# A four-layer conditioned network: pass change, first stagings, tail, store order and demodulation rearranged

## What is computed

```python
# layers 0 and 1 (attention); s1, s2 are halves of the conditioning
xn = normalise(x * s1)
q_dc = rsqrt(einsum('oi,bi->bo', q_weight**2, s1**2) + 1e-8)      # and k, v, w, u
q, k, v = (xn @ q_weight.T) * q_dc, (xn @ k_weight.T) * k_dc, (xn @ v_weight.T) * v_dc * s2
out = softmax(q @ k.T / 4) @ v
x = x + (out @ w_weight.T) * w_dc + (v @ u_weight.T) * u_dc

# layers 2 and 3 (state space), D_INNER 512, D_STATE 16
xr, gate = split(x @ W_in.T);  xr = xr + cond
xn = layernorm(silu(conv4(xr))) * ln_g + ln_b
Bm, Cm, dt = split(xn @ W_xproj.T)
Ad = 1 - 0.01 * tanh(dt @ W_dt.T + b_dt) * tanh(A_log)
Bd = Bm * min(norm(xn), 1)
for t in range(64):
    h = clip(h * Ad[t] + Bd[t] * xn[t], -10, 10)                  # 64 x 16 x 512
    y[t] = Cm[t] @ h
x = x + ((y + D * xn) * silu(gate)) @ W_out.T
```

## Time and profile before

| | us |
|---|---|
| median of 3 runs | 1900.43 |
| lowest, highest | 1898.62, 1903.49 |
| the profiled execution | 1892.64 |
| its span in the trace | 1890.8 |
| PE / DVE / ACT / POOL busy | 1702.5 / 1654.7 / 1313.4 / 667.1 |
| wait of ACT ahead of `xh` (L880) for the x parts' store, 12 times | 17.8 |
| wait of ACT ahead of `R` (L994) for PE, twice | 13.2 |

### The profile page before, as it was taken

The page is one execution under the profiler, slowest core; times in us unless marked ns, Lnnn a source line. Parts: engine busy times, 40 slices in busy tenths (PEclk is TensorE's granted clock), DMA queues, the critical chain, the costliest instruction groups (busy, mean ns, idle before and its releaser), DMA issues.

```text
span 1890.8 us, 46062 instructions
## 1 busy us (share of the span) xinstructions
PE 1702.5 (90%) x14896; PEld 765.6 (40%) x14896; DVE 1654.7 (88%) x2494; ACT 1313.4 (69%) x2220; POOL 667.1 (35%) x689
## 2 busy tenths in 40 slices
PE   6899899999988999689989998899996899999987
PEld 3555555555553455322222224444452222222243
DVE  3799999999976889989999997569899999999975
ACT  3555455555545888789989991068987899899900
POOL 0223223232321222446656550002225476566400
PEclk9999999999999999799999999999997999899999
DMA  4000000000001334645445658523346454456586
GB/s 153 2 2 0 1 1 30 2 1 0 2 1 78 108 144 177 202 132 160 147 140 189 211 153 253 179 79 140 120 169 204 131 176 145 131 189 216 158 264 237
DMA packets 127189, 228.27 MB, mean 121 GB/s; under 512 B 36085, under 2 KB 61941, under 8 KB 118005
## 3 DMA queue, kind: packets, MB, share of 16 engines
q1 hardware_dynamic: 127064, 226.67, 36.3%
HBM read 143.27 MB, written 83.36 MB: 120 GB/s over the span
## 4 chain that ended last, share of the span: by engine, by line
PE 41%; DVE 24%; ACT 14%; issue 9%; DMA 7%; SPq 3%; DVEq 1%; ACTq 0%
PE PS L1427 9%; PE PS L1410 8%; PE PS L1009 7%; ACT R L994 7%; DVE q L1932 5%; DMA sgp<-sg_d 4%; DVE sm L1564 3%; PE PS L1075 3%; PE PS L1237 3%; DMA xpart_d<-xlo 2%; SPq L328 2%; PE PS L1430 2%; PE PS L1477 2%; ACT ex L724 2%; DVE vare L1505 1%
## 5 line engine op out<-in xcount | busy, mean ns | idle before, releaser
L994 ACT ACTIVATE R<-q,Ast 128x512 f32<-128x512 f32 x1024 | 637.6, 709 | 42.9 <-DVE q L1932 28.1
L1932 DVE SCALAR_TENSOR_TENSOR q<-R,PS 128x512 f32<-128x512 f32 x1008 | 610.0, 676 | 16.8 <-ACT R L994 14.9
L596 POOL TENSOR_TENSOR Uw<-Ub,rowmask 96x512 bf16<-96x512 bf16 x256 | 337.4, 1349 | 188.8 <-PE PS L1410 175.7
L1410 PE MATMUL PS<-xq,Uw 97*128 97x512 bf16 x1024 | 329.1, 397 | 47.2 <-DVE q L1932 39.6
L1427 PE MATMUL PS<-q,Wy 128*32 128x512 f32 x2016 | 283.5, 617 | 1.2 <-DVE q L1932 0.7
L1237 PE MATMUL PS<-X,Win 128*128 (+1 forms) x512 | 239.0, 609 | 4.3 <-DVEq L1715 2.9
L1410 PEld LDWEIGHTS PS<-xq,Uw 97*128 97x128 bf16 x1024 | 85.7, 97 | 367.8 <-DVE q L1932 327.9
L1009 PE MATMUL PS<-xn,Wl 128*128 128x512 f32 x384 | 188.9, 616 | 0.0
L524 POOL TENSOR_TENSOR ex<-ex,rs 128x1024 f32<-128x1024 f32 x32 | 76.9, 2404 | 176.7 <-DVE rs L1567 176.7
L1736 DVE SCALAR_TENSOR_TENSOR acc<-xp,Wc,acc 128x512 f32<-128x512 f32 x192 | 134.6, 748 | 2.5
L1237 PEld LDWEIGHTS PS<-X,Win 128*128 128x128 f32 x512 | 93.1, 192 | 105.2 <-issue 105.2
(11 more groups left out here) (163 smaller groups left out, 2630.4 us busy)
## 6 DMA issues: line engine op xcount, KB each, us to landing
xq<-xpart_d SPq DMA_DIRECT2D x384, 192.0 KB
sg_d<-sg SPq DMA_DIRECT2D x16, 1024.0 KB, 6.7
xn_d<-z SPq DMA_DIRECT2D x16, 1024.0 KB, 5.6
y_d<-ys SPq DMA_DIRECT2D x64, 256.0 KB, 3.9
xnp<-xn_d SPq DMA_DIRECT2D x16, 1024.0 KB, 9.5
sgp<-sg_d SPq DMA_DIRECT2D x16, 1024.0 KB, 12.6
yt<-y_d SPq DMA_DIRECT2D x32, 512.0 KB, 9.1
xpart_d<-xh SPq DMA_DIRECT2D x16, 512.0 KB, 2.9
```

The costliest lines, as they stand in the source:

```text
L596: pl.tensor_tensor(Uw[0:XROWS, h, w, :, :, :], Ub[0:XROWS, w, 0:N, ds(s0, CH)].rearrange("p n t -> p t n").unsqueeze(2).broadcast_to([XROW ...
L994: act.activation(R[:, w, :], q[:, t % 2, w, :], ACT.Relu, scale=Ast[:, h, w, t:t + 1], bias=CLIP).then_inc(ac_r, 1)
L1410: pe.matmul(PS[:, w, :], Uw[0:KROWS, h, w, t, :, :].rearrange("p b n -> p (b n)"), xq[0:KROWS, hb, w, s8 % XT, :], start=True, stop=True). ...
L1932: v.scalar_tensor_tensor(out=q[:, s8 % 2, w, :], in0=R[:, w, :], scalar=2 * CLIP, in1=PS[:, w, :], op0=ALU.min, op1=ALU.subtract).then_inc ...
```

## The change

- **Pass change.** A new buffer `R_end` takes the state after step 63 of pass 0 (ACT's last 4 activations of the pass write it). POOL, no longer DVE, turns it into the clipped state, between `stage(1, 0, 0)` and `stage(1, 0, 1)`. ACT's wait for the last y is gone at the second pass. PE issues the next pass's `inputs` 0 ahead of y 63, `inputs` 1 behind it, and the last y only behind `inputs` 2 of the next pass. At the end of pass 1 DVE still does it in R.
- **First stagings.** POOL waits for `row_r` of the last group ahead of chunk 0's staging (mean rows) and of chunk 1's (deviation rows). PE waits for each `Uw` by itself instead of for all four.
- **Tail.** Most parts of `last_group` come one to two steps later on PE, ACT and DVE. `log_norm` now runs ahead of the switch to the tanh table, so one of the table loads goes.
- **Stores.** In the front the x parts are stored ahead of the B rows, except for group 6.
- **Demodulation.** The second layer's is cut in four, each part in a body (g = 2 to 5) ahead of `largest`; for this DVE's bodies 1 to 4 of the first layer are straight code.

```diff
@@ -193,6 +193,7 @@
 ys = sb("ys", [P, 2, DI], where=scan)
+R_end = sb("R_end", [P, QW, DI], where=scan)
@@ -351,8 +352,8 @@
 store_decay(it, g)
+store_parts(it, g)
 store_b(it, g)
-store_parts(it, g)
@@ -412,14 +413,14 @@
 load_tables(0, (1,))
+store_parts(l * G + QW, QW)
 store_b(l * G + QW, QW)
-store_parts(l * G + QW, QW)
...
 store_decay(l * G + QW + 1, QW + 1)
+store_parts(l * G + QW + 1, QW + 1)
 store_b(l * G + QW + 1, QW + 1)
-store_parts(l * G + QW + 1, QW + 1)
@@ -623,6 +624,8 @@
 for h in range(2):
+    pl.wait_ge(row_r, l * (2 * G) + (2 * AT + 2 * G - 1 + h))
+    alone(pl)
@@ -645,7 +648,13 @@
 alone(pl)
-with pl.Fori(0, CHUNKS // 2) as c2:
+stage(1, 0, 0)
+for p in range(2):
+    pl.wait_ge(ac_r, l * (PASSES * QW * S) + QW * S - QW + 2 * p + 2 + READY)
+    alone(pl)
+    pl.tensor_scalar(R_end[:, 2 * p:2 * p + 2, :], R_end[:, 2 * p:2 * p + 2, :], 2 * CLIP, -CLIP, ALU.min, ALU.add).then_inc(ep_q, 1)
+stage(1, 0, 1)
+with pl.Fori(1, CHUNKS // 2) as c2:
@@ -947,24 +956,24 @@
     std_high(it)
+if n == 2:
     std_middle(it)
-if n in (3, 4):
-    for m in (2 * n - 6, 2 * n - 5):
-        shifted(it, m)
...
     for m in (2 * n - 10, 2 * n - 9):
+        shifted(it, m)
+if n in (7, 8):
+    for m in (2 * n - 14, 2 * n - 13):
         squared(it, m)
-if n == 9:
+if n == 10:
     minus_c(it)
+if n == 11:
     decay_in(it)
-if n == 10:
-    silu_set()
-if n == 11:
-    decay_tanh(it, PS[:, 6, 3 * P:4 * P])
-    logarithm_set()
...
     log_norm(it)
-if n == 16:
+    silu_set()
+if n == 13:
+    decay_tanh(it, PS[:, 6, 3 * P:4 * P])
+if n == 17:
@@ -980,18 +989,18 @@
-def clamp(pi, c2, first, between=None):
+def clamp(pi, c2, first, between=None, end=None):
...
         act.wait_ge(pl_a, cn + 1)
-        if first and h == 0:
+        if first and h == 0 and between:
...
                 act.wait_ge(dv_q, cn * (QW * CH) + QW * t + w + 1 + QW)
-                act.activation(R[:, w, :], q[:, t % 2, w, :], ACT.Relu,
+                act.activation((end if end and (h, t) == (1, CH - 1) else R)[:, w, :], q[:, t % 2, w, :], ACT.Relu,
@@ -999,8 +1008,9 @@
     clamp(pi, c2, c2 == 0, last_group if ps == 0 else None)
-with act.Fori(plain, CHUNKS // 2) as c2:
+with act.Fori(plain, CHUNKS // 2 - 1) as c2:
     clamp(pi, c2, False)
+clamp(pi, CHUNKS // 2 - 1, False, end=R_end if ps == 0 else None)
@@ -1363,23 +1373,23 @@
 it = l * G + G - 1
-if n == 1:
+if n == 3:
...
     spread_out(7, rows3, zb_mm)
-if n == 5:
+if n == 7:
     project_part(it, 2, xd_mm)
-if n == 6:
+if n == 8:
     project_part(it, 0)
-if n == 7:
+if n == 9:
     project_part(it, 1, xw_mm)
-if n == 8:
+if n == 10:
...
         norm(it, m)
-if n == 10:
+if n == 12:
...
     decay(it, PS[:, 6, 3 * P:4 * P])
-if n == 15:
+if n == 16:
@@ -1403,14 +1413,14 @@
         pe.wait_ge(one_in[s8 // 4], l * 32 + 32)
-    if t == 0:
-        pe.wait_ge(pl_u, cn * QW + QW)
     for w in range(QW):
+        if t == 0:
+            pe.wait_ge(pl_u, cn * QW + w + 1)
...
-def y_of(pi, c2, s8, last=False, spare=None):
+def y_of(pi, c2, s8, last=None, spare=None):
@@ -1425,7 +1435,7 @@
 pe.matmul(PS[32 * w:32 * w + 32, 4 + h, :], Wy[:, h, w, t * 32:(t + 1) * 32],
-          R[:, w, :] if last else q[:, s8 % 2, w, :], start=(t == 0), stop=False, skip_group_check=True)
+          last[:, w, :] if last else q[:, s8 % 2, w, :], start=(t == 0), stop=False, skip_group_check=True)
@@ -1435,11 +1445,14 @@
 pi = l * PASSES + ps
-plain = TAIL if ps == 0 else 0
+plain = TAIL if ps == 0 else 1
...
     for s8 in range(1, 9):
-        last_group(c2 * 8 + s8)
-        inputs(pi, c2, s8 + 1, c2 == 0)
+        if ps == 0:
+            last_group(c2 * 8 + s8)
+        inputs(pi, c2, s8 + 1, ps == 0 and c2 == 0)
+        if ps and s8 == 1:
+            y_of(pi - 1, CHUNKS // 2 - 1, 8, last=R_end, spare=(0, 0))
@@ -1448,11 +1461,12 @@
             inputs(pi, CHUNKS // 2 - 1, s8 + 1)
+        elif ps == 0:
+            inputs(pi + 1, 0, 0)
         y_of(pi, CHUNKS // 2 - 1, s8)
-    if ps + 1 < PASSES:
-        inputs(pi + 1, 0, 0)
+    if ps == 0:
         inputs(pi + 1, 0, 1)
-    y_of(pi, CHUNKS // 2 - 1, 8, last=True, spare=(0, 0) if ps + 1 < PASSES else (XB - 1, XT - 1))
+y_of(l * PASSES + PASSES - 1, CHUNKS // 2 - 1, 8, last=R, spare=(XB - 1, XT - 1))
@@ -1607,17 +1621,48 @@
-def demodulation(l):
...
+def all_dco(l):
+    return dco[:, l * 5:l * 5 + 5, :, :].rearrange("p w c b -> p (w c b)")
...
+def dco_step0(l):
     v.wait_ge(dco_g, l + 1)
-    dcv = dco[:, l * 5:l * 5 + 5, :, :].rearrange("p w c b -> p (w c b)")
-    root(dcv, dsq[:, l, :], EPS_DM, dcv, dtm[:, :], dco_r, l * 3)
+    v.scalar_tensor_tensor(out=dtm[:, :], in0=dsq[:, l, :], scalar=EPS_DM, in1=all_dco(l),
+                           op0=ALU.add, op1=ALU.mult).then_inc(dco_r, 1)
...
+def dco_step1(l):
+    v.wait_ge(dco_r, l * 3 + 1)
+    v.scalar_tensor_tensor(out=dtm[:, :], in0=dtm[:, :], scalar=-0.5, in1=all_dco(l),
+                           op0=ALU.mult, op1=ALU.mult).then_inc(dco_r, 1)
...
+def dco_step2(l):
+    v.wait_ge(dco_r, l * 3 + 2)
+    v.scalar_tensor_tensor(out=all_dco(l), in0=dtm[:, :], scalar=1.5, in1=all_dco(l),
+                           op0=ALU.add, op1=ALU.mult).then_inc(dco_r, 1)
...
+def dco_tables(l):
+    v.wait_ge(dco_r, l * 3 + 3)
...
     v.wait_ge(tab_r, l * 2 + 2)
...
+def demodulation(l):
+    dco_step0(l)
+    dco_step1(l)
+    dco_step2(l)
+    dco_tables(l)
...
+def demodulation_piece(l, n):
+    if n == 0:
+        dco_step0(l)
+    if n == 1:
+        dco_step1(l)
+    if n == 2:
+        dco_step2(l)
+    if n == 3:
+        dco_tables(l)
@@ -1657,6 +1702,8 @@
 out_of(it, l, g, 0)
+if l == 0 and g in (2, 3, 4, 5):
+    demodulation_piece(1, g - 2)
@@ -1694,13 +1741,12 @@
 body(l * G, l, 0, 0, (l - 1, G - 1) if l else None, (l, 1), 2)
-with v.Fori(0, 2) as g2:
-    for u in range(2):
-        body(g2 * 2 + (l * G + 1 + u), l, g2 * 2 + (1 + u), 1 - u, (l, g2 * 2 + u),
-             (l, g2 * 2 + (2 + u)), g2 * 2 + (3 + u))
-if l == 0:
-    demodulation(1)
-for g in range(5, G):
+if l:
+    with v.Fori(0, 2) as g2:
+        for u in range(2):
+            body(g2 * 2 + (l * G + 1 + u), l, g2 * 2 + (1 + u), 1 - u, (l, g2 * 2 + u),
+                 (l, g2 * 2 + (2 + u)), g2 * 2 + (3 + u))
+for g in range(5 if l else 1, G):
@@ -1871,22 +1917,24 @@
     inverse_std(it, 6)
+if n == 2:
     std_rest(it)
+if n == 3:
     std_rows(it)
-if n in (2, 3):
-    for m in (2 * n - 4, 2 * n - 3):
+if n in (4, 5):
+    for m in (2 * n - 8, 2 * n - 7):
         gained(it, m, 7)
-if n == 9:
+if n == 11:
     norm_bound(it)
-if n == 13:
+if n == 14:
...
     over_last(it)
-if n == 14:
     inverse_norm(it)
+if n == 15:
...
     carried(it)
-if n == 16:
+if n == 17:
@@ -1954,9 +2002,10 @@
         eight(pi, c2, False, True)
-    for p in range(2):
-        v.wait_ge(ac_r, pi * (QW * S) + QW * S - QW + 2 * p + 2 + READY)
-        v.tensor_scalar(R[:, 2 * p:2 * p + 2, :], R[:, 2 * p:2 * p + 2, :], 2 * CLIP, -CLIP, ALU.min, ALU.add).then_inc(ep_q, 1)
+pi = l * PASSES + PASSES - 1
+for p in range(2):
+    v.wait_ge(ac_r, pi * (QW * S) + QW * S - QW + 2 * p + 2 + READY)
+    v.tensor_scalar(R[:, 2 * p:2 * p + 2, :], R[:, 2 * p:2 * p + 2, :], 2 * CLIP, -CLIP, ALU.min, ALU.add).then_inc(ep_q, 1)
```

## The result

The changed kernel takes 1871.0 us (median of 4 runs, 1870.09 to 1874.95) against 1901.7 for the kernel before (4 runs, 1898.62 to 1903.49): ratio 0.984, 95% interval 0.982 to 0.987, so 30.7 us less. Forecast were 1866 us and 34.4 us less, with a range of 1854 to 1883: inside it, some 5 us too fast.

A forecast was written before the change was run, and what follows sets the result against it. DVE was taken to bound the steady scan, unchanged, with gains only where its pace breaks. Terms 8.7 + 5.5 + 8 + 12.2 = 34.4 us off the 1900.4 median gave 1866 us, range 1854 to 1883.

The forecast's parts named there:

- Demodulation: Attention, between DVE's bodies 4 and 5: the 8.5 us gap goes, plus 0.2 for straight code; 8.7 us (7.2 to 9.4).
- X parts first: Front rounds: four rounds a layer drop from 26.45 to 25.75 us; 5.5 us for both layers (3 to 7).
- Scan's start: Start of each scan: 5.8 us won, 2.1 lost; 4 us a layer, 8 for both (-2 to 12).
- The walk of the queues: Scan's start: four queues followed at 2.54 us a step, putting step 9 near 813.5 instead of 819.28, before a late load.
- The prediction's own sign of being wrong: Scan's start: an SP row of x parts, then PE waiting on the load of x longer than 3 us.
- the collisions: Scan's start: operations moved into POOL's staging at step 15 and `split_b` moved out of one; their costs cancel.
- Pass change: Between passes of each scan: 6.2 and 7.6 us over the pace, less 0.8 each; 12.2 us (8 to 13.8).
- The links: Pass change: ACT's 6.06 us wait for y, DVE's clips ahead of step 0 and PE's late inputs all go.
- I take 1.6 each, between 1.4 and 2.3: Pass change: us for each of POOL's two 128x1024 clip operations, done between 974 and 977 and so hidden.
- rival 2: Pass change gives half, because PE's doubled y or POOL's turn shows in steps 2 to 8: 1872 us; chance 0.06.
- at most 11.5 us apart: Sign of being right: copies of y at the pass change at most this far apart for a chunk.
- PE's doubled y: Pass change: PE has two y in one step, after inputs 2, some 1.2 us more; about 0.8 us of delay.

The follow-up runs named there:

- the run with one operation: The changed kernel with POOL's clip of the end buffer cut to the minimum alone, the constant not taken off: 1868.77 us, ratio 0.9836.
- the clip shared: The changed kernel with group 6's x parts stored later, POOL clipping groups 0 and 1 and DVE groups 2 and 3: 1854.13 us, ratio 0.9767.
- The two comparisons of totals: The whole changed kernel against the kernel before, measured first at ratio 0.984 and again on another chip at 0.9845.

## Why the prediction was right, and where not

**Demodulation**, predicted 8.7: the gap went as worked out (8.45 of 8.5), and the products are at 0.28 us. Straight code was taken at 0.2 in favour; it gives 1.15 in the bodies and takes 2 behind them (5.2 in the first trace). Net 7.6 with the 2.

**X parts first**, predicted 5.5: 5.1, rounds of 25.8 where 25.75 was taken. That the wait of 17.8 us is not the gain held.

**Scan's start**, predicted 8: 6.4 between the two traces, 5.5 by the means. That POOL beside DVE made step 1 late is borne out by all traces: `std_rest` takes 3.87 us in both layers of the five traces with POOL's old order and 0.34 or 0.35 in the nine with the new one. The walk of the queues held to a few tenths up to the load. Placed on the old clock (the front row is 3.9 us earlier now), the deviation rows end near 792, ACT's step 4 starts at 798.0, `xlo` ends at 803.1 against 803.3, the load arrives at 812.1 against 811 to 812.

Two steps of it failed, in opposite directions. First, PE waits 3.85 us (3.46 in the fourth layer), not 2.1, and its clock behind the wait was not counted. Of the 7.4 us that are won ahead of the first copy (44.79 us from the front row instead of 52.19) nothing is left at the second in the third layer (63.23 against 63.21), and 1.2 us in the fourth (62.02 against 63.25). The prediction's own sign of being wrong, a PE wait on this load of over 3 us, did appear. Step 9 was forecast at 813.5 + 2.1 = 815.6 and came at 818.6 on the old clock. Second, the collisions do not cancel. Two operations of `split_b` that took 1.17 and 1.31 us beside POOL's `Uw` take 0.23 and 0.29 out of the staging, and one of the moved operations takes 1.01 beside an `Uw`; the next interval between copies is 2.35 us shorter. (For group 6 it is the other way: the same two operations, ahead of step 0, take 0.66 and 1.31 us instead of 0.27 and 0.39.) That the term came out within 2.5 us is partly luck: both halves were mis-sized and offset each other.

**Pass change**, predicted 12.2: 7.9, or 7.5 by the means. This is the mis-sized term. The links went as said, ACT's 6.06 us wait is gone. The step that failed is "I take 1.6 each, between 1.4 and 2.3": it measured 3.67, outside the bounds. "One input is fewer than two" was no ground for a lower price: the run with one operation has 2.77 us, more than POOL's two-input operations of the same size, which stood in the page of the kernel before:

```profile
L524 POOL TENSOR_TENSOR ex<-ex,rs 128x1024 f32<-128x1024 f32 x32 | 76.9, 2404 | 176.7 <-DVE rs L1567 176.7
L517 POOL TENSOR_TENSOR vsc<-vTd,vs_t 128x1024 f32<-128x1024 f32 x16 | 41.1, 2571 | 228.0 <-ACT vTd L712 228.0
```

The second operation adds 0.86, and the row from which the lower end came was another engine's. So POOL is done at 978.8 on the old clock and not between 974 and 977, and rival 2, POOL's turn, became true in part: 3.6 + 4.3 is 65% of the term. The "at most 11.5 us apart" held for two intervals of four. What PE's doubled y costs by itself is not isolated. With the clip shared the two intervals are 0.6 us over the pace in the fourth layer, where 0.8 was taken, and 2.1 over it in the third, where the granted clock is 0.88 and 0.97 instead of 1.00.

The sum of the stretches between the two traces is 29.0 us, less the 2 given back behind the bodies, 27; with the means it is 25 to 26. The two comparisons of totals gave 30.7 and 29.4, with intervals that begin at 25.7 and 24.9. So a difference is not certain. If there is one, it may lie in the part behind the last scan, which the change does not touch: it takes 85.1 to 88.0 us in the eight traces with at least three of the parts and 84.6 to 92.5 in the six others, 86.4 and 89.4 in the mean. That is not explained. All four terms were forecast at or above what was measured, so the total was some 5 us too fast; the range held because it was added up from wide bounds.

The Trainium skill ("SBUF — State Buffer", Who interferes with whom) was weighed against the 3.87 us row. The rows beside POOL's `Uw` fit a bound of one POOL instruction: 1.17, 1.31 and 1.01 us for operations of 0.23 to 0.29 are each less than one `Uw` of 1.35 more. (The 1.17 is a cast with one input, of which the rule on two inputs does not speak.) The 3.87 us beside `xlo` do not fit it, and they are no single event: all ten rows of that form with POOL's old order have 3.87 or 3.88. The operation is 3.5 us longer than without POOL, three times one `xlo` of 1.15. Here the bound of one POOL instruction does not hold; what decides between the two cases no run shows.
